# An attention and FFN block on one core: output product in float16 pairs, new orders, tiled first products

## What is computed

```
q = LN(x) @ wq (32 heads, 128 of 192 columns used)   k, v = LN(x) @ wkv (32 heads x 128)
scores = q @ k.T * 192**-0.5, causal;  attn = softmax(scores) @ v
x = x + attn @ wo
h = relu(s0 * LN(x) @ (+-1)) * 2;  h = relu(s1 * ei(h) @ (+-1)) * 2
x = x + s2 * ei(h) @ (+-1)          # ei: the last fifth of the channels times -4
```

## Time and profile before

| | |
|---|---|
| median of 3 runs | 1138.96 us (1137.42 to 1138.97) |
| the profiled execution, its time | 1138.74 us |
| its span, first to last instruction | 1136.9 us |
| TensorE, VectorE, ScalarE, GpSimd busy | 1092.0, 895.9, 678.0, 667.6 us |
| granted TensorE clock, mean | 0.998 |
| wait that ends most idle time of TensorE | GpSimd's split of wqk, then the low half of attn |

### The profile page before, as it was taken

The page is one execution under the profiler, slowest core; times in us unless marked ns, Lnnn a source line. Parts: engine busy times, 40 slices in busy tenths (PEclk is TensorE's granted clock), DMA queues, the critical chain, the costliest instruction groups (busy, mean ns, idle before and its releaser), DMA issues.

```text
span 1136.9 us, 18752 instructions
## 1 busy us (share of the span) xinstructions
PE 1092.0 (96%) x6223; PEld 655.2 (58%) x6223; DVE 895.9 (79%) x1797; ACT 678.0 (60%) x1334; POOL 667.6 (59%) x682
## 2 busy tenths in 40 slices
PE   4989999999999999999999999999999999999998
PEld 2545656565555655555565655556565555656577
DVE  6887787877788787878778787877878778787873
ACT  5865666565565666556566655656565665655453
POOL 2257665657667565765756566576656667664300
PEclk9999999999999999999999999999999999999999
DMA  5454556565465565555556545636565553655401
GB/s 157 88 99 84 119 108 128 100 116 94 96 112 109 121 114 114 82 117 109 91 121 114 124 82 119 112 76 121 117 130 89 117 107 81 118 93 115 92 1 75
DMA packets 367584, 118.25 MB, mean 104 GB/s; under 512 B 313088, under 2 KB 361344, under 8 KB 367488
## 3 DMA queue, kind: packets, MB, share of 16 engines
q1 hardware_dynamic: 367488, 117.05, 52.5%
HBM read 39.39 MB, written 2.12 MB: 37 GB/s over the span
## 4 chain that ended last, share of the span: by engine, by line
PE 75%; DVE 12%; issue 6%; ACT 4%; POOL 3%; DMA 0%; SPq 0%; POOLq 0%; ACTq 0%; DVEq 0%
PE psC L1108 42%; PE psS L1108 16%; PE psC L1231 16%; DVE p L975 3%; DVE qk L907 2%; POOL wqk L487 2%; ACT raw L674 2%; POOL wqk L484 1%; DVE res L991 1%; DVE attn L958 1%; ACT attn L728 1%; DVE bound L930 1%; DVE psS L968 0%; DVE bound L936 0%; DVE bound L933 0%
## 5 line engine op out<-in xcount | busy, mean ns | idle before, releaser
L1108 PE MATMUL psC<-xb,wqk 128*128 128x512 f16 x1356 | 328.1, 381 | 12.5 <-POOL wqk L487 10.9
L706 ACT ACTIVATE psS<-psS,negmax 128x128 f32<-128x128 f32 (+7 forms) x256 | 182.8, 714 | 221.3 <-DVE negmax L968 220.4
L1108 PE MATMUL psC<-wos,attn 128*128 128x512 f32 x768 | 253.5, 441 | 13.5 <-DVE attn L958 10.1
L968 DVE CUSTOM_DVE_ANT_0 psS<-psS,mask,undo_qk 128x128 f32<-128x128 f32 (+7 forms) x256 | 208.4, 820 | 62.2 <-PE psS L1108 60.5
L975 DVE SCALAR_TENSOR_TENSOR p<-psS,p 128x128 f16<-128x128 f32 (+7 forms) x256 | 192.6, 752 | 60.2 <-ACT p L714 57.1
L1108 PE MATMUL psS<-qkT 128*128 128x512 f16 (+3 forms) x1152 | 230.0, 327 | 1.2 <-DVE p L975 0.7
L1108 PEld LDWEIGHTS psC<-xb,wqk 128*128 128x128 f16 x1356 | 124.5, 98 | 160.3 <-issue 36.3
L1231 PE MATMUL psC<-pT,v 128*128 128x512 f16 (+3 forms) x1152 | 197.8, 326 | 0.0
L991 DVE SCALAR_TENSOR_TENSOR res<-psC,rinv,res 128x512 f32<-128x512 f32 x256 | 190.1, 743 | 9.3 <-DVE rinv L982 8.1
L1108 PE MATMUL psC<-wvs,xb 128*128 128x256 f16 x1536 | 188.5, 273 | 0.4 <-POOL wvs L487 0.4
L484 POOL TENSOR_TENSOR wqk<-raw,one 128x512 f16<-128x512 f32 x122 | 115.9, 950 | 110.4 <-ACT raw L674 97.8
(11 more groups left out here) (89 smaller groups left out, 936.0 us busy)
## 6 DMA issues: line engine op xcount, KB each, us to landing
raw<-in_L_attn_wkv SPq DMA_DIRECT2D x64, 256.0 KB, 3.4
raw<-in_L_attn_wq SPq DMA_DIRECT2D x32, 256.0 KB, 3.7
raw<-in_L_attn_wo SPq DMA_DIRECT2D x32, 256.0 KB, 3.5
pT<-p SPq DMA_TRANSPOSE x256, 4.3
wrow<-wmax_rows SPq DMA_DIRECT2D x45, 64.0 KB, 4.7
res<-in_L_attn_hidden_states SPq DMA_DIRECT2D x8, 256.0 KB, 6.0
...
```

The lines of the kernel that those rows point to most:

```text
L706: nc.scalar.activation(row, row, ACT.Exp, bias=negmax[:, n:n + 1], scale=-1.0, accum_out=rowsum[:, j % 2, n:n + 1]) \
L968: nc.vector.tensor_tensor_reduce(row, row, mask[:, S - width:S], undo_qk[:, j % 2:j % 2 + 1], 3e38, ALU.add, ALU.min, negmax[:, n:n + 1]). ...
L1108: last = nc.tensor.matmul(out_ap, w, x, start=k == 0, stop=k == len(terms) - 1)
```

## The change

Five things change together:

1. `attn` and `wos` are float16 pairs. wo gets its own squares, bound and scaling once a pair (`mx2`, `sc2` for the first pair, `r2`); the values' and wo's bounds travel together (`put1`, `get1`) after the first pair. Both heads of wo are loaded at once.
2. The attention leaves PSUM as float32 on ScalarE (`keep_pv`, step `pv`), is rounded to its high half by ScalarE (`attention_hi`, step `ah`), and its low half is made by GpSimd (`attention_lo`, step `al`) in place of VectorE's `pv_lo`. The scales of v and wo are undone in `rinv`, the factor of the output's sum (two small operations on VectorE in place of one).
3. The DRAM transfers of row sums (`put`, `get`) are issued on ScalarE's queue; the transposes stay on SyncE's.
4. `y0` to `y3` become `ya` and `yb`, products of one row tile each (12 matmuls with 128 columns), so that they may begin when their tile is split. TensorE runs 10 and 24 matmuls of `ident` by `ident` ahead of the first transposes (WARM).
5. All orders and BANKS are new.

```diff
-    pv1@-1 s4@0 v0@0 s5@0 v1@0 x3@1 v2@0 s6@0 v3@0 x4@1 s7@0 x5@1 o4@-1 x6@1 o5@-1 x7@1 v4@0 o6@-1 x1@2 v5@0 s0@1
-    x2@2 o7@-1 s1@1 pv0@0 s2@1 v6@0 o0@0 s3@1 o1@0 v7@0 o2@0 s4@1 o3@0 s5@1 pv1@0 s6@1 x3@2 s7@1 o4@0 x4@2 o5@0 x5@2
-    x6@2 o6@0 x7@2 o7@0 pv0@1 x1@3 o0@1 s0@2 o1@1 s1@2 x2@3 o2@1 s2@2 o3@1 s3@2""", """
-    y0@2 spread1@2 y1@2 spread2@2 turn4@2 turn5@2 turn6@2 turn7@2 v0@2 v1@2 v2@2 s0@2 s1@2 y2@2 s2@2 s3@2 y3@2 v3@2
+    pv1@-1 x3@1 s4@0 x4@1 s5@0 x5@1 o4@-1 x6@1 s6@0 x7@1 s7@0 v0@0 o5@-1 v1@0 o6@-1 v2@0 s0@1 v3@0 x1@2 x2@2 o7@-1
+    pv0@0 s1@1 v4@0 s2@1 v5@0 s3@1 v6@0 o0@0 v7@0 s4@1 o1@0 s5@1 o2@0 pv1@0 o3@0 s6@1 x3@2 o4@0 s7@1 o5@0 o6@0 x4@2
+    o7@0 x5@2 pv0@1 x6@2 x7@2 o0@1 x1@3 o1@1 s0@2 o2@1 s1@2 x2@3 s2@2 o3@1 s3@2""", """
+    spread1@2 ya0@2 yb0@2 ya1@2 ya2@2 yb1@2 spread2@2 ya3@2 turn4@2 v0@2 turn5@2 yb2@2 turn6@2 turn7@2 yb3@2 v1@2
...
-    r1@0 e6@-1 h6@-1 r0@1 e7@-1 h7@-1 qk2@0 pv0@-1 qk3@0 snap0@1 qk1@0 e0@0 h0@0 e1@0 h1@0 mx0@2 e2@0 h2@0 e3@0 h3@0
+    mx1@0 qk0@0 e6@-1 h6@-1 e7@-1 mx0@2 r0@1 h7@-1 pv0@-1 ah0@-1 put0@2 qk3@0 qk2@0 qk1@0 mx2@0 put1@0 e0@0 snap0@1
+    h0@0 e1@0 h1@0 e2@0 e3@0 get1@0 h2@0 pv1@-1 h3@0 get0@2 ah1@-1 e4@0 h4@0 r1@0 e5@0 qk0@1 h5@0 e6@0 h6@0 qk2@1
+    v0@0 r0@2 v1@0 e7@0 qk3@1 v2@0 mx0@3 h7@0 e0@1 v3@0 snap0@2 put0@3 r2@0 qk1@1 pv0@0 h0@1 e1@1 h1@1 ah0@0 v4@0
...
+    nhi0@2 nhi1@2 mx1@2 r1@2 nhi2@2 vhi0@2 keep0@2 keep1@2 nhi3@2 keep2@2 vhi1@2 root1@2 mx0@3 y0@2 nhi4@2 nhi5@2
...
+    m5@0 l4@0 a5@1 o4@-1 l5@0 m6@0 a6@1 m7@0 a7@1 sc0@2 v0@0 l6@0 o5@-1 v1@0 v2@0 m0@1 o6@-1 rv0@0 v3@0 l7@0 m1@1
...
+    qk0@0 wo0@-1 wqk0@1 al0@-1 qk3@0 qk2@0 sum0@1 qk1@0 al1@-1 wv0@0 wv1@0 qk0@1 qk2@1 wqk0@2 wv2@0 qk3@1 qk1@1
+    wo0@0 al0@0 sum0@2 al1@0""", """
...
+WARM = (10, 24)
-BANKS = "301230123012301201230120123012301230123012"
+BANKS = "012301230123012301230123012301230120123012"
...
-            def pv_hi(g, j, c, bank):
+            def keep_pv(g, j, c, bank):
                 wait(act, done["pv"], g, 2, j, c + 1)
+                wait(act, lo_done["pv"], g, 2, j, c - 1)
+                nc.scalar.activation(attn32[:, c, :], psC[:, bank, :], ACT.Copy, scale=PV_DOWN).then_inc(pv_kept, 1)
+
+            def attention_hi(g, j, c):
+                wait(act, pv_kept, g, 2, j, c + 1)
                 wait(act, done["o"], g, 8, j, 4 * c)
+                nc.scalar.activation(attn[:, HI, :], attn32[:, c, :], ACT.Copy) \
                     .then_inc(hi_done["pv"], 1)
...
+            def attention_lo(g, j, c):
+                wait(pool, hi_done["pv"], g, 2, j, c + 1)
+                nc.gpsimd.tensor_tensor(attn[:, LO, :], attn32[:, c, :], attn[:, HI, :], ALU.subtract)                     .then_inc(lo_done["pv"], 1)
...
-                nc.vector.reciprocal(rinv[:, :], rowsum[:, j % 2, :]).then_inc(rinv_done, 1)
+                nc.vector.reciprocal(rowinv[:, :], rowsum[:, j % 2, :]).then_inc(inverse_done, 1)
+                wait(dve, inverse_done, g, 1, j, 1)
+                wait_pair(dve, undo_ready, g, 1, j, 1)
+                nc.vector.tensor_scalar_mul(rinv[:, :], rowinv[:, :], undo_o[:, :]).then_inc(rinv_done, 1)
...
+            def plain_tile(step, t, bank):
+                n = TILED[step, t - t % 4]
+                c, a = n // 2 % 2, (A11, S2)[n % 2]
+                if t % 4 == 0:
+                    pe.wait_ge(plain_lo if n % 2 else first_lo, 1)
+                pe.wait_ge(xt_lo, t + 1)
+                terms = []
+                for d in range(DC):
+                    terms += halves(lambda w: wqk[:, w, a + d // 2, d % 2, :],
+                                    lambda w: xb[:, 2 * c + d // 2, w, d % 2, t % 4 * P:(t % 4 + 1) * P])
+                last = chain(psC[:, bank, t % 4 * P:(t % 4 + 1) * P], terms)
...
             pe.wait_ge(const_ready, 1)
+            for t in range(WARM[0]):
+                nc.tensor.matmul(psT[:, t % 4, 0:P], ident[:, :], ident[:, :], start=True, stop=True)
             spread(0)
+            for t in range(WARM[1]):
+                nc.tensor.matmul(psT[:, t % 4, 0:P], ident[:, :], ident[:, :], start=True, stop=True)
```

More of the change, by code:

```diff
@@ L100, in exists @@
         return False
-    if h == 0 and (step[0] in ("mx", "sc", "r", "put", "get", "lqk", "lv") or step[0] == "wv" and step[2] == 2):
+    if h == 0 and (step[0] in ("lqk", "lv") or step[0] in ("mx", "sc", "r", "put", "get") and step[2] == 0 or step[0] == "wv" and step[2] == 2):
         return False
@@ L123, in group_steps @@
             return [x for x in every if x not in gone]
-        return [x for x in steady if exists(g, x)]
+        late = [("pv", -1, 1), ("ah", -1, 1)] + [("o", -1, t) for t in range(4, 8)]
+        return [x for x in steady if exists(g, x) and x not in late] + [x for x in late if x in steady]
     return [x for x in steady if exists(g, x) and x not in done]
@@ L141, in plan_banks @@
             if step not in CHAINS:
+                continue
+            if step in ("ya", "yb") and n % 4:
+                plan[g, step, j, n] = (plan[g, step, j, n - n % 4][0], None)
                 continue
@@ L598, in pool_steps @@
                         split_out(g, j)
+                    elif step == "al":
+                        attention_lo(g, j, n)
                     elif step == "qk":
@@ L788, in _ @@
             ends = group_steps(SCALAR_ORDERS, NG)
-            assert ends[-1] == ("pv", -1, 1)
-            for step in ends[:-1]:
+            assert ends[-2:] == [("pv", -1, 1), ("ah", -1, 1)]
+            for step in ends[:-2]:
                 scalar_step(NG, *step)
             norm_root(2)
+            scalar_step(NG, *ends[-2])
             scalar_step(NG, *ends[-1])
@@ L916, in bounds @@
             def bounds(g, j, n):
-                at, done_n, per = (2, bounded[1], 4) if n else (j % 2, bounded[0], 5)
+                first = isinstance(g, int) and g + j // GH == 0
+                a, b = (j % 2, j % 2 + 1) if n == 0 else (n + 1, n + 2) if first else (2, 4)
+                done_n, per = bounded[n], 5 if n == 0 else 4
                 w = wait_pair if n else wait
-                total, root, inverse, scale = (bound[:, at, k:k + 1] for k in range(4))
-                if isinstance(g, int) and (GH * g + j <= 1 or n and g + j // GH == 0):
+                total, root, inverse, scale = (bound[:, k, a:b] for k in range(4))
+                if isinstance(g, int) and (n == 0 and GH * g + j <= 1 or n == 1 and first):
                     k = (0, 2)[GH * g + j] if n == 0 else 1
@@ L946, in undo_values @@
                 wait_pair(dve, bounded[1], g, 4, j, 4)
-                wait_pair(dve, lo_done["pv"], g, 2 * GH, j, 0)
-                nc.vector.tensor_scalar_mul(undo_v[:, :], bound[:, 2, 1:2], 2.0 ** (67 - W_UP) / UP).then_inc(undo_ready, 1)
+                if isinstance(g, int) and g + j // GH == 0:
+                    dve.wait_ge(bounded[2], 4)
+                wait(dve, rinv_done, g, 1, j, 0)
+                nc.vector.scalar_tensor_tensor(undo_o[:, :], bound[:, 1, 2:3], 2.0 ** (141 - 2 * W_UP), bound[:, 1, 3:4],
+                                               ALU.mult, ALU.mult).then_inc(undo_ready, 1)
             def v_lo(g, j, n, bank):
@@ L1056, in _ @@
             outs = [x for x in ends if x[0] == "o"]
-            late = ends[ends.index(("pv", -1, 1)):]
-            early = [x for x in ends if x not in late]
-            assert [x[2] for x in late[1:]] == [4, 5, 6, 7]
+            late = ends[-4:]
+            early = ends[:-4]
+            assert late == [("o", -1, t) for t in range(4, NT)]
             for t in range(4):
@@ L1070, in _ @@
                 norm_apply(NT + t)
-            vector_step(NG, *late[0])
             for t in range(4):
                 norm_lo(NT + t)
-            for step in late[1:]:
+            for step in late:
                 vector_step(NG, *step)
@@ L1149, in bank_free @@
                 elif kind == "pv":
-                    wait(pe, lo_done["pv"], g, 2, j, n + 1)
+                    wait(pe, pv_kept, g, 2, j, n + 1)
                 else:
```

172 lines of the change are left out of this document (92 added, 80 removed).

## The result

The changed kernel takes 1196.05 us (median of 4 runs, 1191.55 to 1198.43) where the kernel before took 1138.89 in the same session: a ratio of 1.05, 95% interval 1.0463 to 1.0538. The forecast was 1105 with a range of 1089 to 1122. It is slower by 57 us, and the prediction had the wrong sign.

The account below looks back on a forecast made before the run. TensorE's queue was taken as the bound: 62.4 us of float16 work plus 1.1 of waits make 63.5 a pair, 2.15 less; 15 pairs give 32. 1138.96 - 32 - 1 (start) = 1106, stated as 1105, range 1089 to 1122.

Parts of the forecast that it names:

- Landing stays covered: Row-sum stores and reads moved to ScalarE's queue: put and get many steps apart, so TensorE's cost was counted as nothing.
- Rival 2: ScalarE's queue: DMA issues there cost 1.3 us each, a pair takes 67.7 us, kernel slower at 1168 us; chance 0.05.
- Issuing engines are not separate DMA queues: Skill rule on DMA: another issuing engine saves only issuing time, because all queues run on the same 16 DMA engines.
- Float16: Output product on TensorE in float16 instead of float32r: removes 1.2 us a pair, bounds 1.0 and 2.1.
- (a): Value chain pv0@1 to output product o0@1: 2.6 us of work against a 2.65 us path, a stall of 0.1 to 0.4.
- (b): x1@2 behind s7@0, waiting for split query weights: 6.7 us of work against 6.4, so this stall mostly goes.
- (c): s2@2 needs the low half of the first probabilities, behind several ScalarE steps: 0.2 to 0.5 us late.
- (d): x3@1 and s4@0 need GpSimd's sums, behind al0 and two roundings in one queue: 0 to 0.4 us.
- The sum of the orders: Stalls in a pair of heads: together 0.3 to 1.7 us, taken as 1.1, so a pair takes 63.5 us.
- The start: Before the steady loop: tile products start as each tile is split; start 1 us earlier, bounds -4 and +4.
- The warm-up: 34 dummy TensorE matmuls at the start: products should find the full clock soon, for a delay taken as 0.5 us.

Follow-up runs that it names:

- e8: e5 with one pair of neighbours swapped in SyncE's list, store put0@2 just ahead of the last transpose t7@-1 instead of behind it: 1191.5 us, ratio 1.0461.
- e5: Changed kernel with all stores and reads of row sums on SyncE's queue, put0@2 and put0@3 behind the last transpose: 1140.4 us, ratio 1.0023.
- e11: e5 with one more store for each pair ahead of t7, 64 KB of the mask in rows of 512 bytes: 1145.1 us, ratio 1.0056.
- e1: Changed kernel with all stores and reads of row sums back on SyncE's queue, put0 just ahead of the last transpose: 1194.6 us, ratio 1.0498.
- e2: Changed kernel with only the reads of row sums back on SyncE's queue: 1196.4 us, ratio 1.0506.
- e3: Changed kernel with only the stores of row sums back on SyncE's queue, put0 just ahead of the last transpose: 1193.6 us, ratio 1.0492.
- e6: Changed kernel with stores and reads of row sums left on ScalarE's queue, each store three to six steps later in ScalarE's list: 1216.1 us, ratio 1.0646.
- e7: Kernel before with attn and wos in float16 and nothing else: 1121.5 us, ratio 0.9852.
- e9: e5 with VectorE's bound sc1@0 behind the low half l4@0, and ScalarE's r1@0 later in its list: 1151.9 us, ratio 1.0109.
- e13: e12 with 136 more semaphore instructions on TensorE's queue ahead of its first transposes: 1157.3 us, ratio 1.0167.
- e12: e5 without the 34 warm-up matmuls: 1185.5 us, ratio 1.0432.
- e14: e12 with 68 more semaphore instructions on TensorE's queue ahead of its first transposes: 1139.6 us, ratio 1.0018.

## Why the prediction was wrong, point by point

*The step that failed* is the one on the bounds' transfers: "Landing stays covered: put and get are many steps apart, and no wait for landing is left on SyncE, whose queue holds the transposes; these were not what TensorE waited for, so I count nothing." It looked at who waits for the store, not at what the store does to transfers in flight. In the kernel before, the stores are issued behind the last transpose, and what they hold up is nobody's need; moved to ScalarE's list they go out 2.3 us ahead of t7 in even heads and 3.9 in odd ones. Counted as nothing, it was worth 3.1 us a pair: 47 us of the spans' difference, and 51 (e8) to 56 us (e5) of the medians. The place is shown by e8, the kind of store by e11, the independence of the queue by e1 to e3 and e6. "Landing stays covered" failed too, once the stores had moved behind t7: store, landing, read and landing take 13.7 us in e5, and TensorE waits 17.1 us behind them. And without the late transposes the forecast would still have missed: e5's 1140.4 us lie above the range's 1122.

*Rival 2*, the only one on this side, had the right sign for a reason that did not hold. A DMA issue on ScalarE took 0.33 us, not the 0.44 of the sum, let alone 1.3. The rule weighed there (the Trainium skill, DMA: Bandwidth & Descriptors, "Issuing engines are not separate DMA queues") holds as far as the queue goes: e1 to e3 agree with it. That all queues share 16 engines, which it also says, is what I did not follow to its end.

*Float16.* The mechanism held. 1.2 us a pair, 18 for 15, were in the sum; e7 has 16.2 for the median, and a period shorter by 1.01.

*(a)*: 0.1 to 0.4 us; measured 0.4, and GpSimd's subtraction 1158 ns where 1.16 stood. *(b)*: gone as foreseen. *(c) and (d)* can't be read in the changed kernel, where the transposes hide them; in e5 s2@2 and x3@1 show no wait of note. What took their place was not on the list: s6@0, behind the bound, 0.8 to 1.5 us in the periods read. The pair's store alone takes 7.5 us to land, the read 5.1, and the order leaves less than that sum. e9 shows that the bound can't simply go behind it.

*The sum of the orders.* 63.5 us a pair was forecast with 1.1 us of waits. With late stores most periods are 64.6 to 65.1 us (the others but two within 64.3 to 66.1), against 64.64 for float16 in the old order: the new order won nothing. (b) gave, and the wait behind the bound took.

*The start.* Forecast 1 us earlier, measured 1.6 later in the changed kernel and 0.7 later in e5. Tile products begin at 16.82 us but stand idle 1.33 and 1.87 us for VectorE's halves and ScalarE's squares. The warm-up did not secure the clock: in e5, the 12 matmuls with 128 columns at 23.61 us took 1.31 us, and the same 12 took 0.83 in the changed kernel.

*Left open.* Most of the 17 us between e5 and e13. One transpose in the twelfth period takes 12.6 to 15.1 us in e5, e6, e8, e9 and e12 to e14 (13.2 in e5, worth some 6.7 us there), but 5.6 in e11, with no cause found. And why a store of single elements takes 8 us and slows what is in flight: only that it does.
